# The gate products of x: from DVE steps to transposes and small matmuls inside the first adjacency sweep

## The reference

```
x = x + A @ (norm(x) @ W + b) / deg              A = adj != 0, deg = column sums
x = x + experts(norm(x))                         top 2 of 8 experts, each 256 -> 1024 -> 256, gelu
x = x + relu(adj_norm @ norm(x) @ WL.T + bL)     adj_norm = (adj + I), scaled by degrees
x = x + nibbles(norm(x))                         row-wise, on a few columns
```

## Time and profile before

| | us |
|---|---|
| median of 3 runs | 1023.33 (1023.2 to 1023.76) |
| the profiled execution, its own time | 1023.41 |
| its span | 1021.6 |
| PE busy | 925.5 |
| DVE busy | 628.3 |
| POOL busy, ACT busy | 429.5, 401.2 |

### The profile page before, as it was taken

How to read it: one execution, slowest core, us unless ns; L and a number is a source line. 1 busy time by engine, 2 the same in 40 slices (tenths; PEclk the granted TensorE clock), 3 DMA queues, 4 the chain that set the end, 5 groups by cost and what they waited for, 6 DMA issues and landing times. The chain is left out here.

```text
span 1021.6 us, 21589 instructions
## 1 busy us (share of the span) xinstructions
PE 925.5 (91%) x6509; PEld 605.7 (59%) x6510; DVE 628.3 (62%) x2051; ACT 401.2 (39%) x837; POOL 429.5 (42%) x435
## 2 busy tenths in 40 slices
PE   7999899999913899999999999999379999999994
PEld 4344344544502899989899889889234454444442
DVE  7617999998698655655655656656256141241644
ACT  5868829575896443233233232233013101010111
POOL 4446707704676245545545545545444400210110
PEclk9999999999955999999999999999789999999997
DMA  9999959889786423323322332323299979875770
GB/s 332 404 319 358 365 187 358 323 307 374 263 289 180 162 44 48 53 46 47 53 46 46 54 47 44 56 47 47 44 329 402 371 233 324 272 258 171 241 257 29
DMA packets 91434, 199.92 MB, mean 196 GB/s; under 512 B 14097, under 2 KB 47122, under 8 KB 91250
## 3 DMA queue, kind: packets, MB, share of 16 engines
q1 hardware_dynamic: 74626, 169.41, 47.1%
q0 software_dynamic: 16752, 29.82, 14.5%
HBM read 177.04 MB, written 22.16 MB: 195 GB/s over the span
## 5 line engine op out<-in xcount | busy, mean ns | idle before, releaser
L1006 PE MATMUL bank<-adj_f,feat 128*128 128x512 f16 x1024 | 237.1, 388 | 7.3 <-DMA adj_f<-in_adjT 5.3
L1259 ACT ACTIVATE act_f<-bank,b_sb 128x256 f32<-128x256 f32 (+1 forms) x312 | 122.2, 449 | 255.4 <-PE bank L1190 255.4
L1190 PE MATMUL bank<-rT,experts 128*128 128x256 f16 (+1 forms) x1872 | 191.2, 263 | 2.4 <-DVE rT L1298 2.4
L1202 PE MATMUL bank<-experts,act_h 128*128 (+1 forms) x1680 | 189.1, 273 | 0.0
L1660 PE MATMUL bank<-adj_g,feat 128*128 128x512 f16 x768 | 179.7, 388 | 1.5 <-POOL feat L1486 1.5
L1190 PEld LDWEIGHTS bank<-rT,experts 128*128 (+1 forms) x1872 | 168.8, 99 | 19.8 <-DVE rT L1298 2.9
L1006 PEld LDWEIGHTS bank<-adj_f,feat 128*128 128x128 f16 x1024 | 97.8, 96 | 136.0 <-DMA adj_f<-in_adjT 7.4
L1202 PEld LDWEIGHTS bank<-experts,act_h 128*128 128x128 f16 x1680 | 163.0, 98 | 18.2
L1117 POOL DMA_INDIRECT x_rows<-y,token x70 | 116.0, 1657 | 66.1 <-issue 57.9
L891 ACT ACTIVATE spent<-adj_f 128x1024 f16<-128x1024 f32 x128 | 135.1, 1055 | 13.6 <-DMA adj_f<-in_adjT 6.7
L1660 PEld LDWEIGHTS bank<-adj_g,feat 128*128 128x128 f16 x768 | 74.4, 97 | 94.8 <-issue 2.4
(11 more groups left out here) (261 smaller groups left out, 977.6 us busy)
## 6 DMA issues: line engine op xcount, KB each, us to landing
adj_f<-in_adjT SPq DMA_DIRECT2D x128, 512.0 KB, 7.0
adj_g<-in_adjT SPq DMA_DIRECT2D x72, 512.0 KB, 6.1
adj_early<-in_adjT SPq DMA_DIRECT2D x24, 512.0 KB, 7.0
adj_g<-in_adjT SPq DMA_DIRECT2D x48, 256.0 KB, 3.1
unit_f<-in_W SPq DMA_DIRECT2D x16, 512.0 KB, 6.9
stage<-in_W SPq DMA_DIRECT2D x12, 512.0 KB, 6.2
x_ring<-in_x POOLq DMA_DIRECT2D x16, 256.0 KB, 6.5
x_rows<-agg SPq DMA_DIRECT2D x4, 1024.0 KB, 9.7
```

The costliest lines, as they stand in the source:

```text
L1006: last = pe.matmul(mine(s)[ib * DC + c][:, :], feat0[:, j, h, c * P:(c + 1) * P], adj_0[j % RING][:, ib * HALF_SWEEP:(ib + 1) * HALF_SWEEP ...
L1190: last = pe.matmul(pb[2 + q][:, k * SLOT + at:k * SLOT + at + width], w1_part(mine_e * DC + (f // FQ * W2_UNIT0 + c), wh)[:, (f % FQ) * P: ...
L1202: last = pe.matmul(pb[6 + r][:, 0:D], act_h[:, ah, f, r * P:(r + 1) * P], experts[:, ds(e[r] * DC + (W2_UNIT0 + f // UH), 1), wh, (f % UH) ...
L1259: last = a.activation(act_f[q][:, k, at:at + width], pb[2 + q][:, k * SLOT + at:k * SLOT + at + width], ACT.Gelu, bias=b1_sb[:, ds(mine_e ...
```

## The change

The products on DVE, the turned copy of Wg and its two loads are gone. Instead PE transposes the rows of `feat0` in sweep 0: beginning with tile 20, three rows n to a tile, `transpose_row(n)` (4 transposes of 128 columns into bank 4 or 5) and `gate_row(n - 1)` (4 matmuls with 16 or 8 columns of the centred, split Wg, into bank 6) stand between the pairs of 512-column matmuls of the tile. DVE copies each transposed row from PSUM into one of two buffers (`take_transposed`) and reads all sums at the end (`take_x_gates`). `take_w0T` and `split_w0` stand behind row 5 in DVE's order, `split_w0g` behind row 20. The projections of sweeps 1 and 2 stand behind tiles 4 to 11, those of sweep 3 behind 20 to 27 as before. The x pieces 2, 3 and 4 are issued behind tiles 3, 7 and 12. One small load (`wg_end`) is added to the weights, and 20 matmuls to the 70 ahead of tile 0. Before sweep 1 PE also waits for `xg_read`, and POOL waits for `xT_used` before it loads x again.

```diff
@@ regions
-    wg_turned = w("wg_turned", [P, E, D], F32)
-    wg_rows = w("wg_rows", [P, D // 2, E], F32)
-    products = Region(TURN_AT, TURN_AT + D // 2 * E * 4)("products", [P, PRODUCTS, D], F32)
+    wg_end = w("wg_end", [P, E], F32)
+    wgx = w("wgx", [P, DC, E], F32)
+    wgx16 = w("wgx16", [P, DC, 2, E], F16)
+    xT = [w(f"xT{i}", [P, 2, DC, P], F16) for i in range(2)]
...
-               (wg_sb[:, :, :], Wg.rearrange("(c p) n -> p c n", p=P))]
+               (wg_sb[:, :, :], Wg.rearrange("(c p) n -> p c n", p=P)),
+               (wg_end[:, :], Wg[D - 1:D, :].partition_broadcast(P))]
...
-    ROWS_OUT_AT = 20
+    XT_FROM, XT_EACH, XT_TILES, ROWS_OUT_AT, ROWS_OUT_LAST = 20, 3, NT, 4, 20
-    X_AFTER = {0: 1, 2: 2, 5: 3, 7: 4}
+    X_AFTER = {0: 1, 3: 2, 7: 3, 12: 4}
@@ SP
-                    if (s, j) == (1, 4):
...
-                        load_gate_rows(0)
-                    if (s, j) == (1, 6):
...
-                        load_gate_rows(1)
@@ DVE
+                v.tensor_tensor(wgx[:, :, :], wg_sb[:, :, :], wg_end[:, :].unsqueeze(1).broadcast_to([P, DC, E]), ALU.subtract
...
+                v.tensor_scalar(wgx16[:, :, 0, :], wgx[:, :, :], WS, None, ALU.mult).then_inc(sem("wgx_ready"), 1)
...
-            def turn_gate_rows(h):
-            def total_gate_rows():
-            def x_gates(first, end):
-            def centre_x_gates():
+            def take_transposed(n):
+                v.wait_ge(sem("xT_ps_ready"), n + 1)
+                if n >= 2:
+                    v.wait_ge(sem("xT_used"), n - 1)
+                v.tensor_copy(xT[n % 2][:, :, :, :].rearrange("p h c n -> p (h c n)"), pb[4 + n % 2][:, 0:D].bitcast(F16)
+                              ).then_inc(sem("xT_ready"), 1)
...
-            take_w0T()
-            split_w0()
-            split_w0g()
-            for h in range(2):
-                turn_gate_rows(h)
-            total_gate_rows()
+            for n in range(XT_TILES):
+                take_transposed(n)
+                if n == 5:
+                    take_w0T()
+                    split_w0()
+                if n == 20:
+                    split_w0g()
+            take_x_gates()
...
             for s in (1, 2):
+                low_sums(s - 1)
                 if s == 1:
-                    x_gates(0, 2)
-                    low_sums(0)
                     take_numbers()
-                    x_gates(2, BEFORE)
...
                 for k in range(OT):
                     take_rows((s - 1) * OT + k)
-                    x_gates(done + k, done + k + 1)
...
-            x_gates(done, 2 * NT)
-            centre_x_gates()
@@ PE
+            def transpose_row(n):
+                pe.wait_ge(sem("hid_lo_ready"), n + 1 + 2)
+                if n >= 2:
+                    pe.wait_ge(sem("xT_ready"), n - 1)
...
+                        last = pe.transpose(dst[:, h, c, :], feat0[:, n, h, c * P:(c + 1) * P], ident16[:, :])
+                last.then_inc(sem("xT_ps_ready"), 1)
+
+            def gate_row(n):
+                pe.wait_ge(sem("xT_ready"), n + 1)
...
+                    for h, width in ((0, 2 * E), (1, E)):
+                        last = pe.matmul(pb[6][:, n * 2 * E:n * 2 * E + width], xT[n % 2][:, h, c, :],
...
+                last.then_inc(sem("xT_used"), 1)
...
-            for _ in range(70):
+            for _ in range(90):
...
+                def row_gates(k):
+                    n = (j - XT_FROM) * XT_EACH + k
+                    if k < XT_EACH and n < XT_TILES:
+                        transpose_row(n)
+                    if k < XT_EACH and 0 < n <= XT_TILES:
+                        gate_row(n - 1)
+
+                tile_sums(0, j, row_gates if j >= XT_FROM else None)
...
-                at = ROWS_OUT_AT
+                at = ROWS_OUT_LAST if s == NS - 1 else ROWS_OUT_AT
```

More of the change, by code:

```diff
@@ L479, in _ @@
             pool.wait_ge(sem("spare_zeroed"), 32)
+            pool.wait_ge(sem("w_lo_ready"), 2)
+            pool.wait_ge(sem("w0g_ready"), 2)
+            pool.wait_ge(sem("xT_used"), XT_TILES)
             def load_x_again(m):
@@ L587, in centre_weights @@
                 v.tensor_copy(ident16[:, :], ident[:, :]).then_inc(sem("ident16_ready"), 1)
+                v.tensor_tensor(wgx[:, :, :], wg_sb[:, :, :], wg_end[:, :].unsqueeze(1).broadcast_to([P, DC, E]), ALU.subtract
+                                ).then_inc(sem("wgx_ready"), 1)
+                v.wait_ge(sem("wgx_ready"), 1)
+                v.tensor_scalar(wgx16[:, :, 0, :], wgx[:, :, :], WS, None, ALU.mult).then_inc(sem("wgx_ready"), 1)
+                v.wait_ge(sem("wgx_ready"), 2)
+                v.scalar_tensor_tensor(out=wgx16[:, :, 1, :], in0=wgx[:, :, :], scalar=WS, in1=wgx16[:, :, 0, :],
+                                       op0=ALU.mult, op1=ALU.subtract).then_inc(sem("wgx_ready"), 1)
                 v.wait_ge(sem("wg_sum_ready"), 1)
@@ L621, in x_gates @@
-            def x_gates(first, end):
-                for half in range(first, end):
-                    n = half // 2
-                    for e in range(half % 2 * (E // 2), half % 2 * (E // 2) + E // 2):
-                        k = gate_steps.n
-                        if k >= PRODUCTS:
-                            v.wait_ge(sem("v_gates"), k - PRODUCTS + 1)
-                        gate_steps.did(v.tensor_tensor_reduce(out=products[:, k % PRODUCTS, :], in0=agg[:, n, :], in1=wg_turned[:, e, :], scale=1.0,
-                                                              scalar=0.0, op0=ALU.mult, op1=ALU.add, accum_out=xg[:, n, e:e + 1]))
@@ L631, in centre_x_gates @@
-            def centre_x_gates():
-                v.wait_ge(sem("wg_totalled"), 1)
-                shift = products[:, 0, :].rearrange("p (n e) -> p n e", e=E)
-                gate_steps.wait()
-                gate_steps.link(v.tensor_tensor(shift, over_experts(mv0[:, :, 0]), over_tiles(wg_total[:, :]), ALU.mult))
-                v.tensor_tensor(xg[:, :, :], xg[:, :, :], shift, ALU.subtract).then_inc(sem("xg_taken"), 1)
+            def take_transposed(n):
[4 more added lines that the diff above has]
+                              ).then_inc(sem("xT_ready"), 1)
@@ new lines, in take_x_gates @@
+            def take_x_gates():
+                st = Steps(v, sem("v_xg"))
+                tiles = slice(0, XT_TILES)
+                v.wait_ge(sem("xT_used"), XT_TILES)
+                sums = pb[6][:, 0:XT_TILES * 2 * E].rearrange("p (n h e) -> p n h e", n=XT_TILES, h=2)
+                st.link(v.tensor_copy(xg[:, tiles, :], sums[:, :, 0, :]))
+                v.tensor_tensor(xg[:, tiles, :], sums[:, :, 1, :], xg[:, tiles, :], ALU.add).then_inc(sem("xg_read"), 1)
+                st.link(v.scalar_tensor_tensor(out=t1[:, tiles], in0=var[:, tiles], scalar=1.0 / WS, in1=r[:, tiles], op0=ALU.mult, op1=ALU.mult))
+                v.wait_ge(sem("xg_read"), 1)
+                v.tensor_tensor(xg[:, tiles, :], xg[:, tiles, :], t1[:, tiles].unsqueeze(2).broadcast_to([P, XT_TILES, E]), ALU.mult
+                                ).then_inc(sem("xg_taken"), 1)
@@ L997, in _, with tile_sums @@
             pe.sem_inc(sem("adj_used"), RING)
-            def tile_sums(s, j):
+            def tile_sums(s, j, between=None):
                 pe.wait_ge(sem(f"adj_full{j % RING}"), (s * (NT // RING) + j // RING) * 16 + 16)
@@ L1004, in tile_sums @@
                     for c in range(DC):
+                        if between is not None and h + c:
+                            between(h * DC + c - 1)
                         for ib in range(IB):
@@ L1013, in rows_out @@
                 project(pe, bank[:, 0:W0C], sum_hi, sum_lo, slice(k * P, (k + 1) * P), w0s, W0C).then_inc(sem("agg_ps_ready"), 1)
+            def transpose_row(n):
+                pe.wait_ge(sem("hid_lo_ready"), n + 1 + 2)
+                if n >= 2:
+                    pe.wait_ge(sem("xT_ready"), n - 1)
+                dst = pb[4 + n % 2][:, 0:D].bitcast(F16).rearrange("p (h c n) -> p h c n", h=2, c=DC)
+                for h in range(2):
+                    for c in range(DC):
+                        last = pe.transpose(dst[:, h, c, :], feat0[:, n, h, c * P:(c + 1) * P], ident16[:, :])
+                last.then_inc(sem("xT_ps_ready"), 1)
+            def gate_row(n):
+                pe.wait_ge(sem("xT_ready"), n + 1)
+                k = 0
+                for c in range(DC):
+                    for h, width in ((0, 2 * E), (1, E)):
+                        last = pe.matmul(pb[6][:, n * 2 * E:n * 2 * E + width], xT[n % 2][:, h, c, :],
+                                         wgx16[:, c, :, :].rearrange("p h e -> p (h e)")[:, 0:width],
+                                         start=(k == 0), stop=(k == 3))
+                        k += 1
+                last.then_inc(sem("xT_used"), 1)
             def weight_work(j):
```

33 lines of the change are left out of this document (4 added, 29 removed).

## The result

The changed kernel takes **1031.47 us** in the median (1030.29 to 1032.72, 4 runs) against 1023.55 (1023.2 to 1024.65, 4 runs) of the kernel before on the same chip: ratio **1.0073**, 95% interval 1.0059 to 1.0088. It is slower by 7.9 us; the prediction said 4.9 with a range of 1024.0 to 1034.0.

What follows compares the result with a forecast made beforehand. PE was taken to bound the four sweeps, apart from one wait on DVE in sweep 1 and early loads. -8.0 - 1.4 + 11.0 + 0.3 + 3.0 = +4.9 us on 1023.4 gave 1028.3 us, range 1024.0 to 1034.0.

Steps and rivals of the forecast that it cites:

- The stop: Sweep 1: PE's 6.5 us wait on DVE's copy of a projected row, plus 1.4 for lower clock, goes: -8.0 us.
- The x pieces: Sweep 0: with pieces 3 and 4 loaded later, PE starts tile 13 at 37.9, not 39.3: -1.4 us.
- The warm-ups: Ahead of tile 0: 20 more matmuls take 1.1 us within PE's idle 1.98 us, so cost nothing.
- 32 rows: Tiles 20 to 30 of sweep 0: transposes 0.225 and small matmuls 0.12 us for each row on PE: +11.0 us.
- The hand-over: PE to DVE and back for each transposed row: covered except behind the last row, +0.3 us.
- The wait at tile 22: Sweep 0: PE waits for row 6's copy, queued on DVE behind take_w0T and both splits: +3.0 us.
- The clock behind it: After the tile 22 wait: no clock fall counted, 1.4 us kept for the range.
- Behind the four sweeps: Everything from 272.57 us on only moves with PE, 5 us later, without changing its own length.
- the late hand-over: Rival, 13%: long row copies, slow splits, a clock fall and dearer small matmuls give 1031 to 1037 us.
- the forecast's own 1025.5 to 1032: The main case's span, given 64%, from the bounds of the small matmuls and of the tile 22 wait.

Runs made afterwards that it cites:

- e3_only_x_late: The kernel before with only the x pieces moved, to behind tiles 0, 3, 7 and 12: 1023.63 us, ratio 1.0000.
- e7_filled_wait: The changed kernel with 64 matmuls of 128 columns on zeros ahead of PE's wait for row 6: 1028.05 us, ratio 1.0040.
- e9: The kernel before with 24 DVE gate products moved from ahead of the projected rows to behind them in both sweeps 1 and 2: 1022.66 us, ratio 0.9995.
- e1: The changed kernel with the two splits of w0 behind all 32 row copies in DVE's order, not behind row 5: 1025.13 us, ratio 1.0025.

## Why the prediction was right, and where its sizes were off

Sign and range were right: slower, 1031.5 within 1024.0 to 1034.0. The likeliest value was 3.2 us too low. Point by point:

- **The stop, -8.0:** right, 7.9 from sweep 1 on. No wait of PE on a projected row, granted clock 1.00 from 130 to 140 us.
- **The x pieces, -1.4:** -1.2 by the start of tile 13, -0.9 at the end of the sweeps in e3_only_x_late. But the prediction looked at PE alone. ACT stands for 3.43 and 2.44 us at the roots, and its halves of the weights came 2.8 us later: 1.4 by the late pieces (e3_only_x_late) and 1.4 by the three new steps of DVE on Wg, which the sum has no term for. The step "ACT's halves were done at 56.2, in time" took the old time of an engine whose input the change itself delays.
- **The warm-ups, 0:** right, PE's last wait ahead of its first tile is 0.28 us, where it was 1.98, and the tile starts at 9.33 where it started at 9.39.
- **32 rows, +11.0:** 10.2 by doubling each half, 10.4 by the starts in the changed kernel. The transposes at 0.056 were exact; the small matmuls came out at 0.025 for one, where 0.030 was taken and nothing better than 0.005 and 0.056 bounded them.
- **The hand-over, +0.3:** some 0.1, behind the last row. The copy of 512 f16 elements takes 0.42 us (0.43 taken).
- **The wait at tile 22, +3.0:** 3.96. Of the 4.9 us between w0T's copy and row 6's, 1.06 is waiting for ACT and 2.61 the second split. The prediction took 1.5 for each of the splits from the old trace; here the first took 0.69 and the second 2.61, beside a step of POOL. In the old trace, too, steps of POOL lay beside both splits. A duration read beside another engine's work was used as one that belongs to the instruction.
- **The clock behind it, 0:** this is the term that was mis-sized most, **2.7 us** (e7_filled_wait). Rows of before had 1.88 us without a fall and 6.53 with one; for a gap of 3, and now 3.96, the prediction took the nearer one and kept 1.4 for the range, the price behind the long gap. Here it is double that.
- **Behind the four sweeps:** right, everything moved by PE's 8.2 us, and that part lasts 749.1 us where it lasted 749.0.

The likeliest value was low by what the clock (2.7) and the wait (1.0) cost beyond it, less 0.8 that the rows cost below theirs. The range held because it was made to take in most of the late hand-over.

Of the rivals, the late hand-over was nearest: two of its four parts, the slow splits and the clock, did happen, while copies and small matmuls kept their size. That is why the time fell at its lower edge, and still within the forecast's own 1025.5 to 1032.

## What to carry to other kernels

Where one engine makes another wait, ask before work is moved whether order alone removes the wait or only moves it. Here order alone returned nothing (e9), all of the work moved was a loss of 8 us, still of 2.6 with the splits out of the way (e1), and an eighth of it moved a gain of 7: try first what the length of the wait asks for, not the whole job. And whoever puts a new chain through an engine's queue should go through what already stands in that queue beside it: two splits that nobody had waited for before, now between a copy and its reader, made 6.6 of the 8.2 us at the end of the sweeps. A wait of PE has a second price behind it, in the clock, and moving a load also moves the engines that work on what it brings.
